# One issue list per engine and turn, layer norms applied by ScalarE, and a block inversion that no longer uses GpSimd

## What is computed

```python
def _forward(x, ...):                       # x = layernorm(x), B = 32, T = 256
    q, k, v = (silu(causal_conv(x @ W)) for W in (Wq, Wk, Wv))
    q, k = rope(q), rope(k)
    q = q * rsqrt(sum(q * q) + EPS)         # and k
    beta = sigmoid(x @ bw + bb)
    alpha = exp(-exp(A_log) * softplus(x @ gkw + gkb + dt_bias))
    o = delta_rule(q, k, v, alpha, beta)    # S = a (S - b k kS) + b k v
    o = (x @ Wg) * silu(o * rsqrt(mean(o * o) + EPS) * onorm_w)
    return o @ Wo
x = x + _forward(layernorm(x), ...)
x = x + ffn(layernorm(x), ...)              # layernorm, attention, residual,
                                            # layernorm, router, 2 of 8 experts
```

## Time and profile before

| | |
|---|---|
| median of 3 runs | 7063.38 us (7054.64 to 7068.19) |
| span of the profiled execution | 7067.6 us |
| PE busy | 5137.7 us, 73% |
| DVE busy | 4870.4 us, 69% |
| ACT busy | 3485.1 us, 49% |
| POOL busy | 2615.7 us, 37% |
| mean granted TensorE clock | 0.776 of full speed |

### The profile page before, as it was taken

One profiled execution on the slowest core, in us unless ns is written; L12 is line 12 of the kernel. 1 busy time (PEld: TensorE's weight loads), 2 busy tenths in 40 slices (PEclk: granted clock), 3 DMA queues, 4 the chain that ended last, 5 costly groups with the idle time before them and its releaser, 6 DMA issues.

```text
span 7067.6 us, 126933 instructions
## 1 busy us (share of the span) xinstructions
PE 5137.7 (73%) x40448; PEld 3663.3 (52%) x40448; DVE 4870.4 (69%) x11585; ACT 3485.1 (49%) x5995; POOL 2615.7 (37%) x2957
## 2 busy tenths in 40 slices
PE   3677777777767777777777677777777777777776
PEld 2455555555545555555555455555455454555555
DVE  5667777667776677776677776677766777767752
ACT  2345554545554545545555545455444555455533
POOL 3444333344333444333443334343333433334420
PEclk6677877777877878777778778777777787777777
DMA  1000010000010100110000101000100001000001
GB/s 47 8 20 25 24 34 30 28 26 27 27 34 27 31 22 24 34 34 24 28 25 27 34 27 31 25 28 26 34 27 28 25 24 34 30 28 28 25 25 44
DMA packets 214675, 199.48 MB, mean 28 GB/s; under 512 B 13848, under 2 KB 176416, under 8 KB 209696
## 3 DMA queue, kind: packets, MB, share of 16 engines
q1 hardware_dynamic: 213920, 190.01, 8.9%
HBM read 148.02 MB, written 4.19 MB: 22 GB/s over the span
## 4 chain that ended last, share of the span: by engine, by line
PE 41%; issue 23%; DVE 19%; ACT 10%; POOL 6%; DVEq 1%; ACTq 0%; DMA 0%; SPq 0%; POOLq 0%
PE bank L1039 38%; DVE acc L1433 3%; PE bank L1043 3%; DVE NP L1575 3%; DVE tmpb L1602 2%; DVE mx L1684 2%; DVE Gam L1566 2%; ACT acc L854 2%; POOL fo L716 1%; ACT h L1026 1%; ACT L883 1%; POOL QK L816 1%; POOL nrm L728 1%; DVE Gam L1605 1%; ACT acc L877 1%
## 5 line engine op out<-in xcount | busy, mean ns | idle before, releaser
L1039 PE MATMUL bank<-QK 64*128 64x256 f32 (+1 forms) x4096 | 858.2, 427 | 628.9 <-DVE NP L1575 298.3
L1433 DVE SCALAR_TENSOR_TENSOR acc<-bank,conv_w,acc 128x255 f32<-128x255 f32 (+2 forms) x2304 | 931.8, 473 | 379.7 <-ACT acc L854 197.5
L1039 PEld LDWEIGHTS bank<-QK 64*128 64x128 f32 (+1 forms) x4096 | 358.1, 173 | 1059.4 <-issue 378.1
L1026 ACT ACTIVATE h<-bank,b 128x256 f32<-128x256 f32 x1024 | 415.8, 473 | 611.2 <-PE bank L1039 607.5
L854 ACT ACTIVATE acc<-bank,conv_b,conv_w 128x256 f32<-128x256 f32 x512 | 260.8, 559 | 868.6 <-PE bank L1039 716.3
L1039 PE MATMUL bank<-mT,W 128*128 128x256 f32 x2048 | 665.5, 483 | 24.4 <-DMA W<-in_W 22.6
L789 POOL TENSOR_TENSOR frstd<-fmv,neg_half 128x2 f32<-128x2 f32 x96 | 66.8, 696 | 1350.7 <-DVE fmv L1416 1350.7
L1039 PEld LDWEIGHTS bank<-mT,W 128*128 128x128 f32 x2048 | 502.2, 255 | 121.1 <-DMA W<-in_W 24.1
L1039 PE MATMUL bank<-W,h 128*128 128x128 f32 x4096 | 515.7, 280 | 55.4 <-DVE QK L1701 51.4
L810 POOL TENSOR_TENSOR sq<-acc 128x256 f32<-128x256 f32 x256 | 186.4, 728 | 973.7 <-ACT acc L860 973.7
L1039 PEld LDWEIGHTS bank<-W,h 128*128 128x128 f32 x4096 | 490.9, 194 | 105.6 <-DVE QK L1701 63.0
(11 more groups left out here) (227 smaller groups left out, 11769.9 us busy)
## 6 DMA issues: line engine op xcount, KB each, us to landing
W<-in_W SPq DMA_DIRECT2D x512, 256.0 KB, 2.9
QK<-QK SPq DMA_DIRECT2D x32, 1024.0 KB, 5.4
xin<-in_x SPq DMA_DIRECT2D x32, 128.0 KB, 2.2
x<-in_x SPq DMA_DIRECT2D x32, 128.0 KB, 2.2
xnG<-xnT SPq DMA_DIRECT2D x32, 128.0 KB, 2.0
out<-moe SPq DMA_DIRECT2D x32, 128.0 KB, 2.0
NP<-in_c_alpha_sel SPq DMA_DIRECT2D x1, 1024.0 KB, 5.0
Wqkv<-in_Wq SPq DMA_DIRECT2D x1, 512.0 KB, 6.1
```

What stands on the lines that cost most here:

```text
L1026: ins = s.activation(h1[:, n % 2, f, :], ps[:, q, :], ACT.Gelu_apprx_tanh, bias=b1[:, n, f:f + 1])
L1039: return mm(out_, lhsT, rhs, start=first, stop=last)
L1433: v.scalar_tensor_tensor(acc[:, n % 2, m, j:T], ps[:, m, 0:T - j], conv_w[:, kind, c, PAD - j:KT - j], acc[:, n % 2, m, j:T], ALU.mult, AL ...
```

## The change

The table of milestones is replaced by one list of short steps for each engine (`ORDER`) and a table of PSUM banks (`BANK`). The turn is numbered from 0, with the front stage of batch i in turn i and the later stages one turn later each. Set beside the issue order of before, step by step, the lists of PE are the same; those of the others differ only as follows.

- **Norms.** `ln_apply` leaves DVE. DVE computes a shift, `-mean * rstd`, of 128 x 2 (`ln_shift`), and ACT applies scale and shift (`apply`), two instructions of 128 x 128. On DVE the shifts stand right behind the statistics: `shift:0` ahead of head 0, `fshift:0`, `fshift:1` and `fshift:2` behind their `fstat`. On ACT `xln` stands behind the SiLUs of the outputs, `ln1` and `ln2` ahead of the exponentials of the gate, and `ln3` behind the copies of the gates.
- **Inversion.** `eliminate` does all columns up to the diagonal on DVE; the 46 instructions of POOL per turn are gone.
- **POOL order.** `norm:0` moves from ahead of `root:1` to the first place of the next turn, ahead of `nrm` and `rstd`.
- **Waits.** Signals of a bank are one semaphore instead of one per bank and stage; some waits are for one half instead of both (`top`, `cross`, `o`, `cos`), and some are added where the order alone had guaranteed them. `up` is issued and waited for in halves.

```diff
+    "pool": """
+        norm:0@2 nrm:0@1 rstd:0@0 norm:1@2 frstd:0@2 frstd:1@2 X:0@1 vscale:0@1 vscale:1@1 dots:0@0 cos:0@0 sin:0@0
...
+        dots:7@0 cos:7@0 sin:7@0 root:1@1 xs:0@2""",
+    "act": """
+        gelu:0@3 gelu:1@3 osilu:0@2 osilu:1@2 xln:0@0 xT:0@0 gelu:2@3 gelu:3@3 diag:0@1 diag:1@1 yT:0@2 yT:1@2 yT:2@2
+        yT:3@2 vtap:0@1 gelu:4@3 gelu:5@3 ln1:0@2 ln2:0@2 gate:0@0 gelu:6@3 gelu:7@3 diag:2@1 gelu:8@3 gelu:9@3
...
+        silu:7@0 square:7@0 low:2@1 low:3@1 osq:0@1 osq:1@1 g:0@1 g:1@1 g:2@1 g:3@1 ln3:0@2 mT:0@2 ex:0@2 sums:0@0""",
+    "pe": """
+        GT:0@1 alpha:0@1 kk:0@1 alpha:1@1 alpha:2@1 up:0@3 up:1@3 kk:1@1 alpha:3@1 alpha:4@1 xT:0@0 up:2@3 up:3@3
...
+    "dve": """
+        norms:0@1 GT:0@1 stat:0@0 shift:0@0 alpha:0@1 alpha:1@1 kk:0@1 alpha:2@1 kk:1@1 alpha:3@1 kk:2@1 alpha:4@1
...
+        alpha:9@1 kk:8@1 y:1@2 alpha:10@1 kk:9@1 v:0@1 expert:1@3 x1:0@2 alpha:11@1 kk:10@1 fstat:0@2 fshift:0@2
+        gate:0@0 fstat:1@2 fshift:1@2 expert:2@3 alpha:12@1 kk:11@1 fac:2@1 gates:0@0 alpha:13@1 kk:12@1 expert:3@3
...
+        ctx:1@2 rope:4@0 qk:7@0 swap:6@0 rope:5@0 KS:0@1 KS:1@1 o:0@1 o:1@1 x2:0@2 fstat:2@2 fshift:2@2 QS:0@1
+        cross:2@1 cross:3@1 QS:1@1 ms:0@1 swap:7@0 o:2@1 o:3@1 rope:6@0 ms:1@1 rope:7@0 router:0@2 choice:0@2 wT:0@2
...
-                pool.wait_ge(v_blk.sem, v_blk.at(i, 1))
-                for r in range(SPLIT, SB - 1):
-
-                    n, w, signalled = SB - 1 - r, r + 1 - SPLIT, 2 + 2 * (r - SPLIT)
-                    pool.wait_ge(p_blk.sem, p_blk.at(i, signalled))
-                    tmp_ = tmpp.rearrange("p a b -> p (a b)")[:, 0:n * w].rearrange("p (a b) -> p a b", a=n)
-                    g.tensor_tensor(tmp_, Eb[:, r + 1:, r:r + 1].to_broadcast([P, n, w]),
-                                    X[:, r:r + 1, SPLIT:r + 1].to_broadcast([P, n, w]), ALU.mult).then_inc(p_blk.sem, 1)
-                    pool.wait_ge(p_blk.sem, p_blk.at(i, signalled + 1))
-                    g.tensor_tensor(X[:, r + 1:, SPLIT:r + 1], X[:, r + 1:, SPLIT:r + 1], tmp_, ALU.subtract)\
-                        .then_inc(p_blk.sem, 1)
-                    meanwhile(("block", r))
...
+            def apply(out_, x_, rs, shift_, done):
+
+                for t in range(NT):
+                    ins = s.activation(out_[:, t, :], x_[:, t, :], ACT.Identity, bias=shift_[:, t:t + 1],
+                                       scale=rs[:, t:t + 1])
+                ins.then_inc(done.sem, 1)
+
+            def ln_x(k, n):
+                act.wait_ge(v_ln.sem, v_ln.at(k, 4))
+                apply(xn, xin, rstd, shift, a_xn)
...
+            def ln_third(j, n):
+                act.wait_ge(f_ln.sem, f_ln.at(j, 12))
+                apply(hn, x2, frstd, fshift, a_fln)
...
-            def ln_apply(i, x_, mv_, rs, out_, sig, rsig, rk):
+            def ln_shift(i, mv_, rs, shift_, sig, rsig, rk):
+
                 dve.wait_ge(rsig.sem, rsig.at(i, rk))
-                for t in range(NT):
-                    v.tensor_scalar(out_[:, t, :], x_[:, t, :], mv_[:, t, 0:1], rs[:, t:t + 1], ALU.subtract,
-                                    ALU.mult).then_inc(sig.sem, 1)
+                v.scalar_tensor_tensor(shift_[:], mv_[:, :, 0], -1.0, rs[:], ALU.mult, ALU.mult).then_inc(sig.sem, 1)
...
+            def eliminate(i, r):
+                n, w = SB - 1 - r, r + 1
+                dve.wait_ge(v_blk.sem, v_blk.at(i, 1 + 2 * r))
+                if r == 0:
+                    dve.wait_ge(p_blk.sem, p_blk.at(i, 2))
+                tmp_ = tmpb[:, 0:n * w].rearrange("p (a b) -> p a b", a=n)
+                v.tensor_tensor(tmp_, Eb[:, r + 1:, r:r + 1].to_broadcast([P, n, w]),
+                                X[:, r:r + 1, 0:w].to_broadcast([P, n, w]), ALU.mult).then_inc(v_blk.sem, 1)
+                dve.wait_ge(v_blk.sem, v_blk.at(i, 2 + 2 * r))
+                v.tensor_tensor(X[:, r + 1:, 0:w], X[:, r + 1:, 0:w], tmp_, ALU.subtract).then_inc(v_blk.sem, 1)
```

More of the change, by code:

```diff
@@ L104, in uses_of @@
[L104 to L129, removed]
-    if step == "pv":
-        return [] if n % 2 else [(("pv", n // 2), "a_ctx9", n // 2 + 1, 7)]
-    if step == "ctx":
-        return [(("ctx", n), "v_ctx", 2 * n + 2, 5 + n)]
-    single = {"Wo": ("x1_ready", 1, 6), "hT": ("a_hT", 1, 7), "fqk": ("v_part", 2, 5), "fv": ("v_v9", 1, 6),
-              "ctxT": ("a_ctxT", 1, 7), "fWo": ("v_x2", 1, 5), "mT": ("a_hT", 2, 6), "router": ("v_lg", 2, 7),
-              "wT": ("v_wT", 1, 5), "b2": ("v_moe", 1, 6)}
-    return [(step,) + single[step]] if step in single else []
@@ L828, in _ @@
+            turns(pool, STEPS["pool"], {
+                "rstd": root_x, "nrm": lengths, "X": unit, "Dv": direct, "R1": right_side, "QSadd": with_state,
+                "root": root, "norm": normalise, "frstd": root_ln, "xs": two_x, "vscale": scale_values, "dots": dots,
+                "cos": by_cos, "sin": by_sin})
         @block.scalar
@@ L1030, in _, with turned_ctx, turned_m @@
-            turns(act, back, {"front": front, "V": values, "attn": attn, "experts": experts})
+                s.copy(ctx9[:, 2 * half:2 * half + 2, :], pair(bank("pv", half))).then_inc(a_ctx9.sem, 1)
+            def turned_ctx(j, n):
+                act.wait_ge(*full_at(j, "ctxT"))
+                s.copy(ctxT[:], bank("ctxT")[:, 0:T]).then_inc(a_ctxT.sem, 1)
+            def turned_m(j, n):
+                act.wait_ge(*full_at(j, "mT"))
+                if prev(j) is not None:
+                    act.wait_ge(*full_at(prev(j), "h1", 2 * NE - 1))
+                s.activation(mT[:], bank("mT")[:, 0:T], ACT.Identity, bias=ln_gb[:, 3:4], scale=ln_gb[:, 2:3])\
+                    .then_inc(a_hT.sem, 1)
@@ new lines, in router, with gelu @@
+            def router(j, n):
+                act.wait_ge(v_lg.sem, v_lg.at(j, 2))
+                s.activation(ex[:], lg[:], ACT.Exp).then_inc(a_ex.sem, 1)
+            def gelu(j, n):
+                e, half = n // 2, n % 2
+                act.wait_ge(*full_at(j, "h1", n))
+                if e >= 2:
+                    act.wait_ge(*full_at(j, "y", e - 2))
+                elif prev(j) is not None:
+                    act.wait_ge(*full_at(prev(j), "y", NE - 2 + e))
+                ps = pair(bank("h1", n))
+                for q in range(2):
+                    f = 2 * half + q
+                    ins = s.activation(h1[:, e % 2, f, :], ps[:, q, :], ACT.Gelu_apprx_tanh, bias=b1[:, e, f:f + 1])
+                ins.then_inc(a_h1.sem, 1)
@@ new lines, in _ @@
+            turns(act, STEPS["act"], {
+                "xln": ln_x, "xT": turned_x, "gate": gate_exps, "alphas": gate_alpha, "tap": first_tap, "silu": silu,
+                "square": squares_of, "sums": sums_copy, "vtap": first_tap_v, "vsilu": silu_v, "vcopy": values,
+                "diag": diagonal, "upper": upper, "join1": first_join, "join2": second_join, "top": solved_top,
+                "low": solved_low, "S": state, "osq": square, "g": gates, "osilu": silu_o, "yT": turned_y,
+                "ln1": ln_first, "ln2": ln_second, "ln3": ln_third, "hT": turned_h, "rep": repeated,
+                "att": probabilities, "context": context, "ctxT": turned_ctx, "mT": turned_m, "ex": router,
+                "gelu": gelu})
```

1930 lines of the change are left out of this document (931 added, 999 removed).

## The result

| | median, us | to the kernel before | forecast |
|---|---|---|---|
| before | 7065.8 (7054.6 to 7068.5) | 1 | |
| after | 7785.5 (7716.7 to 7858.1) | 1.098, 95% interval 1.093 to 1.103 | 7277, 7150 to 7370 |

The change costs 10% where 3% were forecast.

The account below looks back on a forecast made before the run. It took PE and DVE waiting on each other, with ACT between, as the bound. 7.6 + 2.2 + 1.0 + 0.3 (fshift:2) - 4.2 = +6.9 us per turn, +214 us over 31 turns: 7277 us, range 7150 to 7370.

Parts of the forecast that it names:

- Head, +7.6: Head of the turn: DVE waits for rstd, the shift is held and xT comes later, +7.6 us per turn.
- rival (1): Head of the turn: the shift slips in ahead of norm:1, 5.0 us per turn, 7218 us; chance 0.12.
- rival (2): norm:0 on POOL meets the choice of the experts, +1.9, 8.8 us per turn, 7336 us; chance 0.10.
- (3): DVE is the path through the whole inversion, +4.6 for +1.0, 10.5 us per turn, 7389 us; chance 0.07.
- Heads 11 and 12, +2.2: Heads 11 and 12: DVE waits for frstd and ln1, gate:0 stands behind ln2 on ACT; +2.2 us per turn.
- Inversion, +1.0: Inversion on DVE: longer rows, partly hidden by waits, less what POOL's instructions had cost DVE; +1.0 us per turn.
- End of the turn, -4.2: End of the turn: ln3 on ACT lets PE start at 3029.3 in place of 3033.53, -4.2 us per turn.
- `norm:0` at nothing: End of the turn: norm:0, 4.25 us, costs nothing, since POOL idles for 8.42 us ahead of nrm.
- The waits and lists: Added waits and the split of up cost sequencers at most 0.8 us together; counted as 0 per turn.
- DVE's 4 us: Sign at the head: DVE idle for about 4 us ahead of the shift in each turn, waiting for rstd.
- the shift of 2: Sign at the head: the shift of x on DVE is near 2 us long.
- the turn of 220 us: Sign for the whole loop: a turn takes 220 us after the change.

Follow-up runs that it names:

- e1: Changed kernel with the shift of x on DVE moved from ahead of head 0 to behind head 1: 7705 us, ratio 1.090.
- e4: Kernel before with the inversion done by DVE alone, POOL's 46 instructions gone, nothing else changed: 7089 us, ratio 1.004.
- e15: e8 with the third norm on ACT, only the last four GELUs' waits exchanged, and the inversion on DVE alone: 6984 us, ratio 0.988.
- e2: Changed kernel with norm:0 on POOL back ahead of root:1 of the same turn: 7826 us, ratio 1.107.
- e17: e15 with norm:0 at the head of the next turn, as the change has it: 7063 us, ratio 1.000.
- e9: Changed kernel with the two waits exchanged for the last four GELUs of a turn only: 7382 us, ratio 1.044.
- e8: Changed kernel with norms back on DVE, inversion shared with POOL, norm:0 back and all GELU waits exchanged: 7163 us, ratio 1.014.
- e13: e9 with the shift of x behind head 1 as well: 7263 us, ratio 1.027.
- e6: Changed kernel with all GELU waits exchanged, the shift of x behind head 1 and norm:0 back ahead of root:1: 7229 us, ratio 1.022.
- e18: e15 with rstd ahead of nrm on POOL at the head of a turn: 6963 us, ratio 0.986.

## Why the prediction was wrong, by its steps

- **Head, +7.6: right.** Measured +7.9 at `xT`; the shift was held in nearly every turn (median 1850 ns), so rival (1) is out. e1 gives 7.4 of it back in its short turn. The pair on ACT takes 0.86 us where 0.9 was taken from rows; the estimate from the page "VectorE: DVE Perf Modes" of the Trainium skill was 0.59, and the measurement decides.
- **Slips in the sums.** The head's own terms give 12.93 - 5.39 = 7.5, not 7.6. The upper bound, rival (2) with half of (3), is 7336 + 56 = 7392, not 7370. Neither matters beside 7785.
- **Heads 11 and 12, +2.2: somewhat low.** PE goes from 9.4 us late at `v:0` to 12.4 at `alpha:14`, +3.0, with slower products in it.
- **Inversion, +1.0: not contradicted.** 0.4 to 1.5 alone (e4), and a gain in e15, where the clock's pattern is another.
- **End of the turn, -4.2: right** (5.85 to 1.45). **`norm:0` at nothing: wrong.** POOL's idle time covers it, but DVE's choice does not stand beside it for free; rival (2) happened in every turn and cost 2.8 us, not 1.9 (e2: 4.0, e17: 2.5).
- **"The waits and lists: 0 ... at most 0.8 together; no row shows them": this step failed.** I priced an added wait by what a sequencer needs for it and never asked in front of which instruction it lands. In the compiled loop one of the GELU's two waits landed ahead of the table load and put five loads per turn behind the products, and two of them, 0.75 and 1.28 us of idle time, are worth 404 us (e9). The rest of this term is not nothing either: with norms, inversion, `norm:0` and the GELU's waits all undone, the lists still cost 1.4%, 93 us (e8).
- **A step that the sum did not have: the clock.** Every duration of PE was taken from rows of before and kept. With two loads late by 2 us together the 17 us at 1.2 GHz ahead of the joins became 27, and in 16 of 27 turns another 34 us followed. Long turns are (16 x 13.7) / 27 = 8 us of the mean turn; the short turn is 17.1 us longer than before, where the sum has 6.9, 2.8 for `norm:0` and 6.9 for the last GELUs (232.1 - 225.2), which is 16.6. That these add up is no proof of the parts: in e13 and e6 they do not.

Of what would show each step, DVE's 4 us, the shift of 2, `xT` at 13 us and `hn` 1 us behind the last copy all came (3074.43 + 0.58 to 3075.84); the turn of 220 us did not.

The rule of the Trainium skill ("SBUF — State Buffer", Who interferes with whom) held for the shift (1.85 us) and the choice of the experts (1.98 us); beside `nrm`, which reads SBUF too, DVE was not held (e18).

Not settled: why the clock falls in the middle of a stage in which PE never stands, and only behind a long stretch at 1.2 GHz; why some kernels run in one even turn and others wander; why the stretch ahead of the joins is long in half of e8's turns; why the compiled loop has a register instruction between the two waits in the one kernel and not in the other. The sum of stalls gave the length of a turn as long as the pattern of clocks stayed (e1, e2: the short turn), but neither the time nor, in e2, even its direction.

## What to carry to other kernels

Ask of every wait that is added or reordered which instruction carries it, and whether something that could run early, such as a table load, now stands behind it. Where TensorE's clock moves between its levels, read the turns one by one before believing a mean: a stall of a microsecond can decide the clock of the stages around it (e9), and an edit that shortens a turn can cost time (e2). Filling PE's waits with products that nobody reads is a cheap test of whether the clock carries a loss.
